# The third choice of experts ahead of the last rotations, and twelve idle products among the second rows

## The reference, cut to what matters

```
h = emb(x) + b + pe
h = h + gelu(2 * Re(scan(lambda, norm(h) @ B) @ C) + D * norm(h))
logits = norm(h) @ router_w.T + router_b; pick the top 2 of 8
h = h + sum over the two experts of weight * ((silu(h1) * h2) @ fc2 + b2)
```

## Time and profile before

| | |
|---|---|
| executions, us | 191.54, 192.73, 193.65 |
| the profiled execution | 190.8 us, span from first to last instruction 189.0 us |
| mean granted TensorE clock | 0.818 of full speed |
| PE, busy | 132.8 us (70% of the span) |
| PE weight loads, busy | 105.0 us (56%) |
| DVE, busy | 112.4 us (59%) |
| ACT, busy | 77.3 us (41%) |
| POOL, busy | 91.0 us (48%) |

### The profile page before, as it was taken

How to read it: one execution, slowest core, us unless ns; L and a number is a source line. 1 busy time by engine, 2 the same in 40 slices (tenths; PEclk the granted TensorE clock), 3 DMA queues, 4 the chain that set the end, 5 groups by cost and what they waited for, 6 DMA issues and landing times.

```text
span 189.0 us, 3503 instructions
## 1 busy us (share of the span) xinstructions
PE 132.8 (70%) x805; PEld 105.0 (56%) x805; DVE 112.4 (59%) x472; ACT 77.3 (41%) x245; POOL 91.0 (48%) x113
## 2 busy tenths in 40 slices
PE   0273169998869879751991269999996979867910
PEld 0021116758559458541981169988886978765300
DVE  4975159599894896840660027755665665542484
ACT  2223216145182152842542065656555656554000
POOL 5777850000574674573267634645554645446200
PEclk9998555897885975996589559999999999999555
DMA  4222147050151431422133113332310100100297
GB/s 137 69 57 56 47 120 168 3 164 3 27 215 42 129 113 43 101 68 70 45 89 85 55 29 98 102 87 72 100 34 32 36 22 28 42 28 27 75 363 230
DMA packets 15093, 15.65 MB, mean 83 GB/s; under 512 B 2995, under 2 KB 11701, under 8 KB 15074
## 3 DMA queue, kind: packets, MB, share of 16 engines
q1 hardware_dynamic: 10914, 9.39, 18.5%
q0 software_dynamic: 2784, 5.28, 8.8%
q10 hardware_dynamic: 1376, 0.77, 1.3%
HBM read 9.62 MB, written 6.27 MB: 84 GB/s over the span
## 4 chain that ended last, share of the span: by engine, by line
PE 48%; DVE 24%; another core or an unknown queue 10%; issue 9%; ACT 6%; DMA 1%; DVEq 0%; ACTq 0%
PE bank L1238 9%; PE bank L1214 8%; PE bank L1224 8%; PE bank L1204 8%; PE bank L1056 7%; PE bank L1258 3%; DVE stats L626 2%; DVE res L841 1%; DVE zst L613 1%; PE bank L1030 1%; DVE res L624 1%; ACT xT L957 1%; ACT ysb L986 1%; ACT w1b L932 1%
## 5 line engine op out<-in xcount | busy, mean ns | idle before, releaser
L355 POOL DMA_INDIRECT sorted_rows<-rows,slot x32 | 32.2, 1005 | 42.4 <-DVE slot L656 33.8
L753 DVE SCALAR_TENSOR_TENSOR act_h<-bank,w1b,sil 128x128 f32<-128x128 f32 x78 | 23.6, 344 | 33.7 <-ACT sil L966 20.9
L1238 PE MATMUL bank<-w_sb,act_h 128*128 x156 | 26.9, 296 | 11.9 <-ACT ysb L986 10.1
L366 POOL DMA_INDIRECT results<-ysb,dest x22 | 21.7, 985 | 18.3 <-ACT ysb L986 11.6
L1238 PEld LDWEIGHTS bank<-w_sb,act_h 128*128 128x128 f32 x156 | 21.5, 200 | 14.3 <-issue 13.8
L1224 PE MATMUL bank<-xT,w1b 128*128 128x128 f32 x156 | 25.8, 292 | 5.1 <-issue 4.1
L966 ACT ACTIVATE sil<-bank,w1b 128x128 f32<-128x128 f32 x78 | 24.7, 375 | 6.1 <-PE bank L1214 4.4
L1214 PE MATMUL bank<-xT,w1b 128*128 128x128 f32 x156 | 25.7, 290 | 0.0
L366 POOL DMA_INDIRECT results<-ysb,xt x17 | 17.2, 1009 | 17.6 <-ACT ysb L986 15.3
L1224 PEld LDWEIGHTS bank<-xT,w1b 128*128 128x128 f32 x156 | 22.3, 206 | 5.5 <-issue 4.3
L957 ACT COPY xT<-bank 128x128 f32<-128x128 f32 x39 | 10.4, 268 | 33.1 <-PE bank L1204 18.5
(11 more groups left out here) (232 smaller groups left out, 200.2 us busy)
## 6 DMA issues: line engine op xcount, KB each, us to landing
w_sb<-w_all SPq DMA_DIRECT2D x8, 386.0 KB
xt<-sorted_rows SPq DMA_DIRECT2D x39, 65.0 KB, 1.8
yres<-results SPq DMA_DIRECT2D x8, 256.0 KB, 4.0
sorted_rows<-pad SPq DMA_DIRECT2D x1, 520.0 KB, 6.1
sorted_rows<-rows,slot POOLq DMA_INDIRECT x32
out<-res SPq DMA_DIRECT2D x2, 256.0 KB, 3.3
results<-ysb,dest POOLq DMA_INDIRECT x22
results<-ysb,xt POOLq DMA_INDIRECT x17
```

Source lines behind the costliest of these rows:

```text
L355: gp.indirect_dma_start(sorted_rows[:, :], bass.IndirectOffsetOnAxis(ap=slot[:, k, t:t + 1], axis=0), rows[:, k, t, :], None).then_inc(s_s ...
L366: gp.indirect_dma_start(results[:, :], bass.IndirectOffsetOnAxis(ap=target, axis=0), ysb[i][:, :], None, bounds_check=bound, oob_is_err=Fa ...
L753: v.scalar_tensor_tensor(act_h[i % 2][:, q], ps_l[sides(i)][:, q], w1b[i % 4][:, 2 * HID + 2 + c:2 * HID + 3 + c], sil[i % 2][:, q], ALU.a ...
L1238: ins = te.matmul(ps_o[sides(i)][:, 0:D], act_h[i % 2][:, c * P:(c + 1) * P], w_sb[:, bass.ds(at + W1 + c * D, D)], start=(c == 0), stop=( ...
```

## The change

Three edits. On DVE, `early_table(0)` and `choose(2)` move from behind the fourth `scan` to a place inside it, between the scan instruction and the two rotations. On PE, `positions(2)` and `count_rows(1)` move ahead of `rotated(3, 0)` and `rotated(3, 1)`. And PE gets twelve more idle products: three behind `turn_u(2)`, six behind `skipped(2)` and three behind `logits(1)`.

```diff
@@ def scan(g), DVE
                 step(v.tensor_tensor_scan(zst[:, :], decay[:, :], zin[:, :], 0.0, ALU.mult, ALU.add))
+                if g == NG - 1:
+                    early_table(0)
+                    choose(2)
                 if g >= 1:
                     dve.wait_ge(s_y, 2 * g)
                 v.tensor_tensor(by_batch(zrot[:, 0, :]), by_batch(zst[:, :]), cos_b, ALU.mult).then_inc(s_zrot, 1)
@@ DVE's list
             scan(3)
-            early_table(0)
-            choose(2)
             find_slots(2)
             early_counts(1)
             add_gelu(3)
@@ PE's list
             turn_u(2)
+            idle_products(3, ps_xT[1])
             b_times_u(2)
             skipped(2)
+            idle_products(6, ps_xT[1])
             turn_x(1)
             logits(1)
+            idle_products(3, ps_xT[1])
             rotated(2, 0)
             turn_u(3)
             rotated(2, 1)
@@ PE's list
             idle_products(1, ps_vs)
+            positions(2)
+            count_rows(1)
             rotated(3, 0)
             rotated(3, 1)
-            positions(2)
-            count_rows(1)
             idle_products(3, ps_vs)
             find_ends(1)
```

## The result

The changed kernel takes 198.88 us (median of 4, 198.63 to 200.76) against 192.72 us before (median of 4, 191.54 to 193.65). The ratio is 1.034, with a 95% interval from 1.027 to 1.042: 6.2 us slower, where 189.7 was forecast. The profiled execution took 200.76 us, with a span of 199.0 us, against 190.8 and 189.0; its difference of 10 us is larger than that of the medians, so places are compared in it, not totals.

A forecast was written before the change was run, and what follows sets the result against it. PE held about half the chain, DVE a quarter, unexplained time a fifth. Part A's -1.7 and part B's -1.3 us moved group 2's scatters and the stall's end by -3.0: 192.7 - 3.0 = 189.7 us, range 187.8 to 193.4.

The forecast's parts named there:

- Part A: Twelve idle products on PE keep the clock high over group 2's rotated products, so DVE's scan ends 1.7 us earlier.
- the 4.64 us: PE's rotated products and transposes of group 2 at the low clock, forecast to become 2.6 us at the high clock.
- The cap that I named myself: ACT's copy of `uT` starts only at 60.25 us, 0.9 us behind its transposes, which could limit part A's gain.
- holds: Waits read as ACT held up until POOL's transfers have drained, ending 1.15 to 1.75 us after a burst's last scatter.
- The rule on idle gaps: Skill's advice to keep PE's idle gaps short; by it the clock would not have fallen and part A would give -0.3.
- Part B: Third choice ahead of DVE's rotations: alone, first gate 2.2 us later, `find_slots(2)` and group 2's scatters 1.3 us earlier.
- my own stall theory: ACT's 6.00 us wait before its copy at 88.53 ends when POOL's burst drains, so it ends 3.0 us earlier.
- The other branch: `find_slots(2)` directly behind the rotations: slot at 75.0 instead of 76.24, 1.3 us earlier, and group 2's scatters with it.
- Rival 3: At DVE's queue at 70.96 the rotations wait 2.2 us for the choice: slower, 194.9 us; chance 0.14.

The follow-up runs named there:

- held-back scatters: Kernel before with POOL holding group 2's eight scatters until PE finished `second(0)`: 196.38 us against 192.27, ratio 1.020.
- the two splits: Changed kernel with group 1's last four or last two scatters held behind the third choice: 192.19 and 194.06 us, kernel before 191.31, on a chip with holds.

## Why the prediction was wrong

**Part A, the clock.** Right as to the mechanism: the clock stayed at 2.4 GHz, and the 4.64 us became 2.5. Wrong as to what it brings: I took 1.7 us because DVE's wait was longer than that. The cap that I named myself, ACT's copy of `uT`, was what held: in the kernel before, the changed kernel and the products alone it started at 60.25, 60.99 and 59.96 us, each 1.2 to 1.4 us after the last scatter of group 0 had ended, though PE's transposes were done 0.9, 2.5 and 2.5 us before it. I had read that same copy as evidence for holds, and did not apply it to part A. On a chip without holds the products alone gave a ratio of 0.991, some 1.4 us, not clear of no change.

**The rule on idle gaps.** The clock fell before although the gap was short, and it did not fall with ordinary products put beside the transposes. With that the reading of the Trainium skill (TensorE: Matmul & The Clock Gate, "Part 4: PE-mode transpose") agrees, that transposes don't count as busy in the same way; its advice on idle gaps alone ("Why this matters for your kernels") would have left part A without an effect on the clock. The runs don't prove the reason, since the products also filled the gap itself: PE's idle time in front of `turn_x(1)` went from 1.18 to 0.33 us.

**Part B, the price.** This is the step that failed: "there is 0.1 us of new wait at most". It was 3.12 us, of which 0.36 passed before PE had made the tile list (71.27, where 70.8 was forecast). I had looked for what DVE waits for and found it finished at 70.8; I had not asked whether a finished result would be seen at once in the tail of POOL's burst (72.96 in the changed kernel), where my own stall theory said that it would not be. In the kernel before DVE spent that time on the rotations, which need nothing new from PE, and took the tile list only at 72.17. The change moved two handshakes with PE ahead of them. The other terms held: the choice took 1.9 us in front of the rotations (3.1 and 1.9 make the 5.0 us), and without a hold the rotations start 3.2 us after the scan's start, of which 1.2 are the scan.

**The other branch.** I forecast slot 1.3 us earlier from the order, and 3.0 with A; it came 1.4 us later (77.42 against 76.02), since it stands behind the same rotations.

**The stall.** The reading was right for this wait: held-back scatters take it with them, and it ends 1.0 to 1.8 us after them, where the burst has drained. It is no rule for every wait. In the kernel before DVE's wait at 103.62 and in the changed kernel the gate's at 86.43 ended inside a burst, and the tile list was taken between 0.9 us before the end of the burst (kernel before) and 1.07 us after it. The waits that lasted until the burst had drained are against what the Trainium skill (DMA: Bandwidth & Descriptors, "SWDGE vs HWDGE vs iDMA") says of a DMA engine, that it takes its queues in turn, as far as that rule reaches to reports between engines. What the forecast missed is that such a wait is not a fixed gate which absorbs lateness: work that had been in front of it fell behind it, so that a burst 1.3 us later cost 4.6 us at `xnT`.

**The rivals.** Rival 3 had the right sign and place (the rotations wait for the choice), at 2.2 us; it lacked the hold, and the range that ended at 193.4 left it out, though it stood at 194.9 with a chance of 0.14. On the chips with holds the loss is 6.2 to 6.7 us.

Not settled: what differs between the chips. The kernel before takes 191 to 193 us in three of the five comparisons and 154 in two, with the same instructions. Nor is it settled through what path a burst delays a report, or why it delays some and lets others through. Held-back scatters take away both the transfers and POOL's work of issuing them, so no run tells the two apart. And what the 1.9 us of the choice cost on a chip with holds is open: the two splits still stand 0.9 and 2.7 us above the kernel before, neither clear of no change.

## What to carry to other kernels

Where a trace shows waits that no instruction released, find what they begin and end with before moving anything near them, and then ask of every handshake that a change moves whether it now falls inside such a stretch: a result that is ready is not yet one that is seen. Work that needs no answer from another engine is what belongs there; in the kernel before the rotations ran there, with the handshakes behind them. A gain behind a wait of this kind should be costed at nothing until the wait itself is shown to move.

## What the runs showed of the hardware

The same kernel took 192.3 us on one chip and 154.0 on another. On a chip with holds, ACT and DVE have waits without a releaser in every part of the span, the longest of 8.73 us in the kernel before. Most lie in or shortly behind runs of POOL's indirect DMAs, but POOL sends these through much of the span, so that nearness alone shows little; the runs with held-back scatters do. SP's issues of tile loads during the burst of group 2 change too, first in the kernel before and then in the changed kernel on the 154 us chip (min, median and max in ns).

```profile
L265 SPq DMA_DIRECT2D xt<-sorted_rows x9: 4/333/691, 74.8 to 88.4; - x9
```

```profile
L265 SPq DMA_DIRECT2D xt<-sorted_rows x13: 333/333/343, 62.2 to 77.7; - x13
```

With holds the median issue is the same 333 ns, but single ones take up to 691 ns; without, none takes over 343 ns.
